# Comparing two Morton curves while the Hilbert keys are computed: one block for keys and ranks

## The chip, the cores and the metric

The kernel runs on one core of a Trainium2 chip. The metric is the device time of one execution in microseconds. TensorE (PE in the profile) multiplies matrices, VectorE (DVE) and ScalarE (ACT) work on tiles of 128 partitions, GpSimd (POOL) and SyncE (SP) are the others; transfers are issued from SP's and ACT's queues here.

## What is computed

The reference is a large model block: a graph attention over points, a Mamba block and a small feed-forward. The change touches its very first step alone, the sorting of 512 points in each of 16 batches along four space-filling curves:

```python
q = _quantize(coords_bn3)                 # 10 bits for each of 3 coordinates
qt = q[..., jnp.array([1, 0, 2])]
keys = [_morton_key(q), _morton_key(qt), _hilbert_key(q), _hilbert_key(qt)]
return [jnp.argsort(kk, axis=1) for kk in keys]
```

A Morton key interleaves the bits of x, y and z. A Hilbert key first transforms the coordinates bit by bit, nine rounds of and, or, xor and shifts, and then interleaves. The kernel doesn't sort: it computes for each point its rank, the number of points of its batch with a smaller key. Later stages gather neighbours by these ranks.

## The kernel before

B = 16 batches, N = 512 points, M = 4 methods (0 and 1 Morton, 2 and 3 Hilbert, each with x and y in order and swapped), NT = N / 128 = 4 tiles of points.

`norm_and_keys` (L93 to L349) is one block. DVE quantizes the coordinates (L237 to L261). SP stores the codes q to DRAM and loads them back over 128 partitions (L177, L179). DVE meanwhile does the layer norm of the latents (L266 to L273), for which ACT takes one square root (L224); SP stores the result to `f0` (L182). Then DVE copies the codes into A for the four methods (L285), works out the Hilbert transform for methods 2 and 3 (L286 to L311), and for all four methods together spreads the bits, puts the keys together and splits each into three parts in 16 bits (L313 to L329). SP stores all keys to `scratch["pk"]` (L185) and, after it has landed, SP loads methods 0 and 1 and ACT methods 2 and 3 into `mv_key` and `st_key` (L165): 16 transfers of 32 KB, each to one partition. The tile `p16` also has a row with the index (L172), four small loads. Eight transfers of 64 KB with constant rows ("units") go to the same two tiles from ACT's queue (L221), ahead of the square root in ACT's order. TensorE folds a convolution into two weight matrices (L195 to L203); DVE scales them after the keys (L331 to L343), TensorE transposes them (L208), DVE copies them (L348, L434, L435).

`ranks` (L352 to L420) is a second block. The four rows of a method lie on partitions 32m to 32m + 3. A product of four rows (L391), the sum of two halves, gives in a PSUM bank of 128 x 512 the difference of the keys of 128 points to all 512. Its sign is what counts: ACT takes methods 0 and 2 by `Sign` with a running sum (L419), DVE methods 1 and 3 by "less than" with a running sum (L406). A pair of comparisons, one for ACT and one for DVE, is issued together, half 0 of both and then half 1 of both:

```python
for half in range(2):
    for m in (2 * pair, 2 * pair + 1):
        last = nc.tensor.matmul(diff[:, t % 2, m, :],
                                st_key[32 * m:32 * m + 4, half, b, t * 128:t * 128 + 128],
                                mv_key[32 * m:32 * m + 4, half, b, 0:N],
                                start=half == 0, stop=half == 1)
```

There are 16 x 4 x 2 = 128 such pairs, 256 comparisons, 512 matmuls. A pair waits until ACT and DVE have both finished with the banks it writes (semaphores `signed`, `counted`); ACT and DVE wait for `compared`. At the end DVE turns ACT's sums into ranks (L409). The order on each engine is that of the code; `wait_ge` holds up all that is behind it on its engine. `link` makes each DVE instruction wait for the one before it. After the block, each block's semaphores are cleared, and `gather_windows` begins (its memsets on POOL, L557 on, its product of tokens, L622).

Of the kernel before, what the change touches and what calls it, by code (L numbers as in the profile page):

```python
# [6 lines left out]
F32 = mybir.dt.float32  # L7
F16 = mybir.dt.float16
# [84 lines left out]
def norm_and_keys(nc, io, scratch, mv_key, st_key, keys_in, weights, latn, fixed):  # L93

    with ExitStack() as ctx:
# [41 lines left out]
        pw = ctx.enter_context(nc.psum_tensor("pw", [128, 2, 4, 512], F32))  # L137
# [17 lines left out]
        turned = sem("w_turned")  # L155
        v_chain = sem("v_chain_keys")
# [3 lines left out]
        def load_keys(eng, m):  # L160

            for r in range(2):
                row = scratch["pk"][m, 2 * r:2 * r + 2, :].rearrange("(r h) (b n) -> r (h b) n", h=2, b=B)
                for tile, at in ((mv_key, 32 * m + r), (st_key, 32 * m + 2 + r)):
                    eng.dma_start(tile[at:at + 1, :, :, 0:N].rearrange("r h b n -> r (h b) n"), row).then_inc(keys_in, 16)  # L165

        @block.sync
        def _(sp):
            sp.dma_start(co[:, :], io["coords"]).then_inc(co_in, 16)
            sp.dma_start(lat[:, :, :], io["x"].rearrange("(t p) d -> p t d", p=128)).then_inc(lat_in, 16)  # L170
            for m in range(4):
# [4 lines left out]
            sp.wait_ge(q_ready, 1)  # L176
            sp.dma_start(scratch["q"], ci[:, :]).then_inc(q_out, 16)  # L177
            sp.wait_ge(q_out, 16)
            sp.dma_start(qin[:, :, :], scratch["q"].rearrange("(k b) n -> k (b n)", k=3)  # L179
                         .rearrange("k (p i) -> p k i", p=128)).then_inc(q_in, 16)  # L180
# [3 lines left out]
            sp.wait_ge(keys_ready, 3)  # L184
            sp.dma_start(scratch["pk"].rearrange("m r (p i) -> p (m r) i", p=128),  # L185
                         p16[:, :, :, :].rearrange("p m r i -> p (m r) i")).then_inc(keys_stored, 16)
            sp.wait_ge(keys_stored, 16)
            for m in (0, 1):
                load_keys(sp, m)
# [4 lines left out]
        def _(pe):  # L194
            pe.wait_ge(w_in, 16 * 7)  # L195
            for l in range(2):
                for m in range(M):
                    nc.tensor.matmul(pw[:, l, 0, 0:C], convT[:, l, :],
                                     lin[:, l, 0:128].rearrange("p (c m) -> p m c", m=M)[:, m, :],
                                     start=m == 0, stop=m == M - 1)  # L200
                nc.tensor.matmul(pw[:, l, 0, C:C + 128], convT[:, l, :], lin[:, l, 128:256], start=True, stop=True)
                nc.tensor.matmul(pw[:, l, 1, 0:1], convT[:, l, :], blin[:, l:l + 1], start=True, stop=True)\
                    .then_inc(folded, 1)  # L203
            for l, W in enumerate(weights):
                O = W["O"]
                pe.wait_ge(scaled, l + 1)
                for side in range(2):
                    last = nc.tensor.transpose(pw[:, l, 2 + side, 0:O],  # L208
                                               eff[0:O, l, side, :, :].rearrange("p c m -> p (c m)"), ident[0:O, 0:O])
                last.then_inc(turned, 1)  # L210

        @block.scalar
        def _(act):
# [16 lines left out]
        def _(dve):  # L230
# [51 lines left out]
            for e in range(2):  # L282
                for k in range(3):
                    src = qin[:, (k if e == 0 or k == 2 else 1 - k), :]
                    link(v.tensor_copy(turns[:, e, :, k, :], src.unsqueeze(1).to_broadcast([128, 2, P64])))  # L285
            ax = [A[:, 2:4, k, :] for k in range(3)]  # L286
# [26 lines left out]
            flat = A[:, :, :, :].rearrange("p m k i -> p (m k i)")  # L313
            flat2 = A2[:, :, :, :].rearrange("p m k i -> p (m k i)")
            for shift, mask in ((16, 0x030000FF), (8, 0x0300F00F), (4, 0x030C30C3), (2, 0x09249249)):
                link(v.scalar_tensor_tensor(flat2, flat, shift, flat, ALU.logical_shift_left, ALU.bitwise_or))
                link(v.tensor_scalar(flat, flat2, mask, None, ALU.bitwise_and))
            link(v.scalar_tensor_tensor(key[:, :, :], A[:, :, 0, :], 2, A[:, :, 2, :],
                                        ALU.logical_shift_left, ALU.bitwise_or))
            link(v.scalar_tensor_tensor(kp[:, :, :], A[:, :, 1, :], 1, key[:, :, :],  # L320
                                        ALU.logical_shift_left, ALU.bitwise_or))

            link(v.tensor_scalar(pi[:, 0, :, :], kp[:, :, :], 2 * BITS, None, ALU.logical_shift_right))
            link(v.tensor_scalar(pi[:, 1, :, :], kp[:, :, :], BITS, 2 ** BITS - 1, ALU.logical_shift_right,
                                 ALU.bitwise_and))
            link(v.tensor_scalar(pi[:, 2, :, :], kp[:, :, :], 2 ** BITS - 1, None, ALU.bitwise_and))
            link(v.tensor_copy(pf[:, :, :, :], pi[:, :, :, :]))
            for part, row, unit in ((0, 0, 32.0), (1, 2, 1.0 / 32.0), (2, 1, 1.0)):
                v.tensor_scalar(p16[:, :, row, :], pf[:, part, :, :], unit, None, ALU.mult).then_inc(keys_ready, 1)  # L329

            link(v.memset(eff[:, :, 0, :, :].rearrange("p l c m -> p l (c m)"), 0.0))  # L331
            for l, W in enumerate(weights):
                dve.wait_ge(folded, l + 1)
                link(v.tensor_copy(W["bias"][:, :], pw[:, l, 1, 0:1]))
                link(v.tensor_reduce(W["amax"][:, :], pw[:, l, 0, 0:C + 128], X, ALU.max, apply_absolute_value=True))
                link(v.tensor_scalar(W["amax"][:, :], W["amax"][:, :], 1e-30, None, ALU.max))
                link(v.reciprocal(inv[:, l:l + 1], W["amax"][:, :]))
                link(v.tensor_scalar(both[:, l, :], pw[:, l, 0, 0:C], inv[:, l:l + 1], None, ALU.mult))
# [4 lines left out]
                v.tensor_scalar(eff[:, l, 1, :, :].rearrange("p c m -> p (c m)"), pw[:, l, 0, C:C + 128],  # L343
                                inv[:, l:l + 1], None, ALU.mult).then_inc(scaled, 1)
            for l, W in enumerate(weights):
                O = W["O"]
                dve.wait_ge(turned, l + 1)
                link(v.tensor_copy(W["center"][:, 0:O], pw[:, l, 2, 0:O]))  # L348
                split16(v, link, W["neigh_hi"][:, 0:O], W["neigh_lo"][:, 0:O], pw[:, l, 3, 0:O])  # L349


def ranks(nc, io, scratch, rank, mv_key, st_key, keys_in):  # L352

    with ExitStack() as ctx:
        def sb(name, shape, dt=F32):
            return ctx.enter_context(nc.sbuf_tensor(name, shape, dt))

        used = []  # L360

        def sem(name):
            used.append(ctx.enter_context(nc.semaphore(name)))
            return used[-1]

        sign = sb("sign", [128, 4, N], F16)
        less = sb("less", [128, 4, N], F16)
        tally = sb("tally", [128, 2, B, NT])
        diff = ctx.enter_context(nc.psum_tensor("diff", [128, 2, M, 512], F32))

        used.append(keys_in)
        compared = sem("compared")
        signed = sem("signed")
        counted = sem("counted")
        scaled = sem("scaled_r")
        ctx.callback(clear, nc, used)
        block = ctx.enter_context(nc.Block())

        @block.tensor
        def _(pe):  # L380
            pe.sem_inc(signed, 4)
            pe.sem_inc(counted, 4)
            pe.wait_ge(keys_in, 16 * 6 * M)
            for b in range(B):
                for t in range(NT):
                    for pair in range(2):
                        pe.wait_ge(signed, b * (2 * NT) + (2 * t + pair + 1))
                        pe.wait_ge(counted, b * (2 * NT) + (2 * t + pair + 1))
                        for half in range(2):
                            for m in (2 * pair, 2 * pair + 1):  # L390
                                last = nc.tensor.matmul(diff[:, t % 2, m, :],  # L391
                                                        st_key[32 * m:32 * m + 4, half, b, t * 128:t * 128 + 128],
                                                        mv_key[32 * m:32 * m + 4, half, b, 0:N],
                                                        start=half == 0, stop=half == 1)
                                if half == 1:
                                    last.then_inc(compared, 1)

        @block.vector
        def _(dve):
            v = nc.vector  # L400
            with dve.Fori(0, B) as b:
                for t in range(NT):
                    for m in (1, 3):
                        dve.wait_ge(compared, b * (M * NT) + (t * M + m + 1))
                        dve.wait_ge(counted, b * (2 * NT) + (2 * t + m // 2 + 1))
# [1967 lines left out]
```

## Time and profile before

| | |
|---|---|
| median of 3 runs | 2323.17 us (2320.01 to 2326.31) |
| the profiled execution | 2328.78 us, its span 2327.0 us |
| keys, from the start to the first comparison | 99.60 us |
| ranks | 99.60 to 179.42 us |
| busy over the span | PE 81%, DVE 82%, ACT 69%, POOL 43% |

In the profile, a name such as "L391 PE MATMUL diff<-mv_key,st_key 4*128 4x512" is the line, the engine, the operation, what it writes and reads, and the shapes: weights of 4 x 128, moving data of 4 x 512. PEld is the loading of weights. A row of the timeline gives the start, the time to the end of what is merged in it, the count (x), and in brackets how long the engine had been idle and what it waited for. SPq and ACTq are the issuing of transfers. PEclk is the clock that the throttle granted to TensorE, as a share of 2.4 GHz.

### The profile page before, as it was taken

What the parts mean: (1) busy time and instruction counts of PE and PEld (TensorE: products, weight loads), DVE (VectorE), ACT (ScalarE), POOL (GpSimd) and SP (SyncE); (2) the same over time, 40 slices, a digit from 0 to 9 for tenths busy, and PEclk for the clock granted to TensorE, in tenths of its full rate; (3) what the DMA queues carried; (4) which work ended last, traced back from release to release, by engine and by line L of the source; (5) the groups of instructions that cost most, each with busy time, mean ns of one, the idle gap of its engine ahead of it and who ended that gap; (6) DMA issues with size and microseconds to landing.
All of it is one profiled execution on the core that took longest, in us unless ns stands there. A gap on an engine that the chain in (4) does not pass through costs nothing. (4 is left out here: it accounts for less than half of the span.)

```text
span 2327.0 us, 99837 instructions
## 1 busy us (share of the span) xinstructions
PE 1877.7 (81%) x37528; PEld 1288.0 (55%) x37528; DVE 1903.8 (82%) x3658; ACT 1616.3 (69%) x3249; POOL 1008.0 (43%) x995
## 2 busy tenths in 40 slices
PE   0296656888888566499999998577999999999948
PEld 0023335777777343389999996333544454445422
DVE  6798986999999599678989987874888888888854
ACT  0299986888888599689999997355455555555422
POOL 0000006999999100268787885002434344434401
PEclk9997668999999666699999998899999999999968
DMA  2103766555555177655555552202222222222110
GB/s 59 14 1 91 166 163 141 122 121 122 123 124 107 35 169 165 156 106 104 109 107 106 110 104 54 83 19 89 86 78 81 78 85 80 81 74 88 48 46 18
DMA packets 435513, 216.09 MB, mean 93 GB/s; under 512 B 301259, under 2 KB 404843, under 8 KB 435304
## 3 DMA queue, kind: packets, MB, share of 16 engines
q1 hardware_dynamic: 430120, 210.73, 38.2%
q10 hardware_dynamic: 5312, 4.31, 0.8%
q8 instruction: 47, 0.77, 0.1%
q14 instruction: 34, 0.28, 0.0%
HBM read 161.97 MB, written 52.96 MB: 92 GB/s over the span
## 5 line engine op out<-in xcount | busy, mean ns | idle before, releaser
L865 PE MATMUL pQ<-QM,QX 128*128 128x64 f16 (+1 forms) x5760 | 531.3, 217 | 2.1 <-issue 2.1
L863 PE MATMUL pQ<-neigh_lo,QX 128*128 128x32 f16 (+1 forms) x5760 | 519.6, 188 | 2.8 <-issue 2.8
L863 PEld LDWEIGHTS pQ<-neigh_lo,QX 128*128 128x128 f16 x5760 | 494.7, 103 | 6.5 <-issue 4.0
L865 PEld LDWEIGHTS pQ<-QM,QX 128*128 128x128 f16 x5760 | 486.6, 104 | 1.3 <-issue 1.2
L961 POOL TENSOR_TENSOR Dm<-Sc,mx 128x450 f32<-128x450 f32 x384 | 365.9, 953 | 79.9 <-DVE mx L921 79.9
L968 POOL TENSOR_TENSOR Ap<-E,R 128x450 f32<-128x450 f32 x384 | 366.0, 953 | 67.8 <-DVE R L934 57.4
L998 ACT ACTIVATE Vs<-pQ 128x480 f32<-128x480 f32 (+1 forms) x384 | 295.6, 770 | 5.4 <-PE pH L891 3.8
L930 DVE STREAM_TRANSPOSE AT<-Ap 128x480 f32<-128x480 f32 x384 | 259.1, 675 | 33.3 <-PE pH L891 10.9
L1963 POOL TENSOR_TENSOR MT<-cb,decay 128x512 f32 (+1 forms) x128 | 164.0, 1302 | 247.8 <-PEq L1731 151.1
L1011 ACT ACTIVATE E<-Dm 128x450 f32<-128x450 f32 x384 | 223.9, 583 | 60.3 <-POOL Dm L961 60.2
L921 DVE TENSOR_REDUCE mx<-Sc 128x15 f32<-128x450 f32 x384 | 223.9, 583 | 15.7 <-ACT Sc L992 15.4
L925 DVE TENSOR_REDUCE Z<-E 128x15 f32<-128x450 f32 x384 | 233.4, 608 | 0.0
L992 ACT ACTIVATE Sc<-pQ 128x450 f32<-128x450 f32 x384 | 208.8, 544 | 14.1 <-PE pQ L865 13.9
L891 PE MATMUL pH<-AT,Vs 128*32 128x30 f32 x17280 | 178.2, 197 | 48.2 <-DVE AT L930 42.6
L891 PEld LDWEIGHTS pH<-AT,Vs 128*32 128x32 f32 x17280 | 173.6, 110 | 68.3 <-DVE AT L930 42.0
L599 DVE TENSOR_TENSOR QT<-ext,cen 128x1710 f16<-128x1710 f32 x96 | 180.6, 1937 | 28.0 <-ACT ext L687 23.4
L858 PE MATMUL pQ<-maskR,maskL 128*128 128x160 f16 (+1 forms) x960 | 142.2, 246 | 69.0 <-DMA QX<-scratch_q 41.4
L1978 POOL TENSOR_TENSOR sqsum<-sqsum,sq 128x512 f32<-128x512 f32 x56 | 85.6, 1529 | 245.8 <-ACT sq L1824 245.8
L1756 PE MATMUL pO<-Wo,yw 128*128 128x512 f16 x768 | 179.7, 385 | 13.3 <-DVE Wo L1921 13.3
L1738 PE MATMUL pG<-h,W 128*128 128x512 f16 x768 | 178.6, 383 | 8.7 <-DVE W L1945 8.4
L1931 DVE SCALAR_TENSOR_TENSOR cv_m<-pX,taps_m,cv_m 128x496 f32<-128x496 f32 (+2 forms) x192 | 137.6, 717 | 51.0 <-ACT cv_m L1833 33.8
L1738 PE MATMUL pX<-h,W 128*128 128x512 f16 x768 | 176.2, 379 | 0.0
(360 smaller groups left out, 3592.2 us busy)
## 6 DMA issues: line engine op xcount, KB each, us to landing
QM<-scratch_q SPq DMA_DIRECT2D x192, 240.0 KB, 2.7
QX<-scratch_q SPq DMA_DIRECT2D x768, 60.0 KB, 2.4
scratch_q<-QT SPq DMA_DIRECT2D x120, 360.0 KB, 4.8
Wg<-in_in_proj SPq DMA_DIRECT2D x64, 256.0 KB, 2.6
Wh<-in_in_proj SPq DMA_DIRECT2D x64, 256.0 KB, 2.8
Wo<-in_out_proj SPq DMA_DIRECT2D x64, 256.0 KB, 2.6
W_s<-in_in_proj SPq DMA_DIRECT2D x16, 256.0 KB, 2.6
CT<-scratch_c SPq DMA_DIRECT2D x192, 11.2 KB, 2.1
```

The costliest lines, as they stand in the source:

```text
L863: nc.tensor.matmul(pQ[:, p, u // PB, o + 32:o + BW], qx[u], W["neigh_lo"][:, 0:O], start=False, stop=True, skip_group_check=True)
L865: last = nc.tensor.matmul(pQ[:, p, u // PB, o:o + BW], qx[u], qm[u], start=False, stop=True, skip_group_check=True)
L891: last = nc.tensor.matmul(pH[at0:at0 + 32, p, 32 * u:32 * u + PTS * K], Vs[:, first + slot, u * O + 32 * half:u * O + 32 * half + 32], AT[ ...
L921: v.tensor_reduce(mx[:, p, :], valid(Sc[:, p, :]), X, ALU.max).then_inc(max_ready, 1)
L925: v.tensor_reduce(Z[:, p, :], valid(E[:, p, :]), X, ALU.add).then_inc(summed, 1)
L930: v.transpose(AT[:, k5 % NA, :], A[:, k5 % ND, :]).then_inc(turned, 1)
L961: nc.gpsimd.tensor_tensor(valid(Dm[:, p, :]), valid(Sc[:, p, :]), mx[:, p, :].unsqueeze(2).to_broadcast([128, SUBS, PTS * K]), ALU.subtrac ...
L968: nc.gpsimd.tensor_tensor(valid(A[:, p, :]), valid(E[:, p, :]), R[:, p, :].unsqueeze(2).to_broadcast([128, SUBS, PTS * K]), ALU.mult).then ...
L992: nc.scalar.activation(like(Sc[:, (k - 1) % ND, :], 32, PTS * K), blocks(p, 0, PTS * K), ACT.Copy)\
L998: nc.scalar.activation(like(Vs[:, kv % RV, :], O, O), blocks(p, 32, O), ACT.Copy).then_inc(vs_ready, 1)
L1011: nc.scalar.activation(valid(E[:, p, :]), valid(Dm[:, p, :]), ACT.Exp, scale=32.0 ** -0.5).then_inc(exped, 1)
L1738: last = nc.tensor.matmul(out, W16[:, i, quarter, a, d, :], h16[:, b, d, :], start=d + a + b == 0, stop=d == DT - 1 and a == 1)
```

## The change

The two functions become one, `keys_and_ranks`, with one block.

- The first Morton methods come first: DVE spreads and splits methods 0 and 1 (`spread(0)`) ahead of the Hilbert transform, and methods 2 and 3 behind it (`spread(2)`). The key store is cut in two, and the key loads follow each: of the first half SP loads method 0 and ACT method 1, of the second SP loads both.
- The comparisons are dealt out anew. ACT takes all of methods 0 and 1 and batches 4 to 15 of method 2: 176. DVE takes batches 0 to 3 of method 2 and all of method 3: 80. The first 96 of ACT's list are issued two by two while DVE works on the Hilbert keys; the other 80 are issued each with one of DVE's.
- PSUM: `diff[:, 0]` is four banks for ACT, `diff[:, 1]` four for DVE. The folded weights lie in two banks of the latter; TensorE transposes them behind the 96, and waits for `taken` before DVE's comparisons write there.
- The eight loads of constant rows go behind the load of q on ACT, and behind the square root; on SP, the small loads (idx, rep, place, ident) go behind it.

```diff
@@ sync @@
             sp.dma_start(lat[:, :, :], io["x"]...).then_inc(lat_in, 16)
+            sp.wait_ge(q_ready, 1)
+            sp.dma_start(scratch["q"], ci[:, :]).then_inc(q_out, 16)
+            sp.wait_ge(q_out, 16)
+            sp.dma_start(qin[:, :, :], ...).then_inc(q_in, 16)
             for m in range(4):
                 sp.dma_start(p16[:, m, 3, :], io["idx"]).then_inc(idx_in, 16)
...
-            sp.wait_ge(keys_ready, 3)
-            sp.dma_start(scratch["pk"]...).then_inc(keys_stored, 16)
-            sp.wait_ge(keys_stored, 16)
-            for m in (0, 1):
-                load_keys(sp, m)
+            for half in range(2):
+                sp.wait_ge(keys_ready, 3 * half + 3)
+                sp.dma_start(scratch["pk"][2 * half:2 * half + 2]...).then_inc(keys_stored, 16)
+                sp.wait_ge(keys_stored, 16 * half + 16)
+                load_keys(sp, 2 * half)
+                if half == 1:
+                    load_keys(sp, 3)
@@ tensor @@
+            def difference(at, bank, m, b, t, half):
+                return nc.tensor.matmul(diff[:, at, bank, :], st_key[32 * m:32 * m + 4, half, b, t * 128:t * 128 + 128],
+                                        mv_key[32 * m:32 * m + 4, half, b, 0:N], start=half == 0, stop=half == 1)
+            def pair(jobs):
+                for at, n, m, b, t in jobs:
+                    pe.wait_ge((signed, counted)[at], n + 1)
+                for half in range(2):
+                    for at, n, m, b, t in jobs:
+                        last = difference(at, n % 4, m, b, t, half)
+                        if half == 1:
+                            last.then_inc(compared[at], 1)
+            signs = [(0, n) + job for n, job in enumerate([(m, b, t) for m in range(3) for b in range(SHARED if m == 2 else 0, B)
+                                                           for t in range(NT)])]
+            counts = [(1, n) + job for n, job in enumerate([(m, b, t) for m in (2, 3) for b in range(SHARED if m == 2 else B)
+                                                            for t in range(NT)])]
+            pe.sem_inc(signed, 4)
+            pe.sem_inc(counted, 4)
+            pe.wait_ge(keys_in[0], 16 * 12)
+            for n in range(0, ALONE * NT, 2):
+                pair(signs[n:n + 2])
             for l, W in enumerate(weights):
                 pe.wait_ge(scaled, l + 1)
...
+            pe.wait_ge(taken, 2)
+            pe.wait_ge(keys_in[1], 16 * 12)
+            for one, two in zip(signs[ALONE * NT:], counts):
+                pair((one, two))
@@ scalar @@
+            act.wait_ge(var_ready, 1)
+            nc.scalar.activation(sd[:, :], mv[:, :, 1], ACT.Sqrt).then_inc(sd_ready, 1)
+            act.wait_ge(q_in, 16)
             for m in range(M):
                 for tile, side, at in ((mv_key, 0, 32 * m + 2), (st_key, 1, 32 * m)):
                     act.dma_start(tile[at:at + 2, :, :, 0:N]..., io["units"][side])\
-                        .then_inc(keys_in, 16)
-            act.wait_ge(var_ready, 1)
-            nc.scalar.activation(sd[:, :], mv[:, :, 1], ACT.Sqrt).then_inc(sd_ready, 1)
+                        .then_inc(keys_in[m // 2], 16)
             act.wait_ge(keys_stored, 16)
-            for m in (2, 3):
-                load_keys(act, m)
+            load_keys(act, 1)
+            def jobs(m, b0, b1, before):
+                with act.Fori(b0, b1) as b:
+                    for t in range(NT):
+                        n = b * NT + (t + before - b0 * NT)
+                        act.wait_ge(compared[0], n + 1)
+                        act.wait_ge(signed, n + 1)
+                        nc.scalar.activation(sign[:, t, :], diff[:, 0, t, :], ACT.Sign,
+                                             accum_out=tally[:, m, bass.ds(b, 1), t]).then_inc(signed, 1)
+            jobs(0, 0, B, 0)
+            jobs(1, 0, B, B * NT)
+            jobs(2, SHARED, B, 2 * B * NT)
@@ vector @@
+            spread(0)
             ax = [A[:, 2:4, k, :] for k in range(3)]
...
+            spread(2)
...
+                dve.sem_inc(taken, 1)
+            jobs(2, SHARED, 0)
+            jobs(3, B, SHARED * NT)
+            dve.wait_ge(signed, (3 * B - SHARED) * NT + 4)
```

`ALONE` is 24 and `SHARED` 4. DVE's `jobs` is as ACT's, with `is_lt`, `diff[:, 1, t, :]`, `compared[1]` and `counted`. `spread(m)` is the code of L313 to L329 on the two methods m and m + 1.

## Rows read from the trace of the kernel before

**Rows 1.** Busy us by stage: PE, PEld, DVE, ACT, POOL, clock, DMA share, GB/s.
```profile
0.00:99.60 99.60, 6.16 (x28) 5.76 (x28) 68.16 (x224) 1.49 (x2) 0.20 (x4) 1.00 0.22 42
99.60:179.40 79.80, 78.21 (x512) 20.47 (x512) 78.44 (x257) 77.75 (x256) 0.00 (x0) 1.00 0.00 1
```
**Rows 2.** Timeline of the keys: start us, us, engine, line, what.
```profile
11.65 0.33 SPq L177 DMA_DIRECT2D scratch_q<-ci  x1
...
29.60 1.53 DVE L285 COPY A<-qin 128x128 int32<-128x128 int32 x6 [8.04 <-DMA qin<-scratch_q]
...
73.90 0.96 DVE L316 SCALAR_TENSOR_TENSOR A<-A 128x768 int32<-128x768 int32 x1
...
80.24 0.43 DVE L318 SCALAR_TENSOR_TENSOR key<-A 128x256 int32<-128x256 int32 x1
...
83.44 0.27 DVE L331 MEMSET eff<- 128x256 f32 x1
...
86.75 0.59 SPq L165 DMA_DIRECT2D mv_key<-scratch_pk  x1
...
99.60 2.00 PE L391 MATMUL diff<-mv_key,st_key 4*128 4x512 f16 x16 [10.96 <-DMA st_key<-scratch_pk]
```
**Rows 3.** Timeline of the ranks: ACT near their start, DVE near their end.
```profile
104.55 0.59 ACT L419 ACTIVATE sign<-diff 128x512 f16<-128x512 f32 x1
...
105.12 0.60 ACT L419 ACTIVATE sign<-diff 128x512 f16<-128x512 f32 x1
...
172.47 0.69 DVE L406 TENSOR_SCALAR_CACHE_REDUCE less<-diff 128x512 f16<-128x512 f32 x1
...
173.08 0.69 DVE L406 TENSOR_SCALAR_CACHE_REDUCE less<-diff 128x512 f16<-128x512 f32 x1
...
179.19 0.23 DVE L409 TENSOR_SCALAR rank<-tally 128x128 f32<-128x128 f32 x1
```
**Rows 4.** TensorE: durations (ns min/median/max), then timeline and clock of two tail stretches.
```profile
L391 PE MATMUL diff<-mv_key,st_key x512: 577/626/630, 99.6 to 177.4; 4*128 4x512 f16 x171
...
L2253 PE MATMUL pu_f<-W_f,uf_f x18: 379/412/635, 2314.7 to 2321.2; 115*128 115x512 f16 x18
...
2302.79 4.00 PE L2253 MATMUL pg_f<-W_f,uf_f 115*128 115x512 f16 x9 [1.37 <-DVE la_f L2182]
...
2319.48 2.12 PE L2253 MATMUL pu_f<-W_f,uf_f 115*128 115x512 f16 x9
...
2302.80:2312.70 9.90, 9.90 (x21) 0.50 0.07 26
...
2318.00:2321.80 3.80, 3.80 (x14) 0.98 0.17 65
```
**Rows 5.** Timeline of two early weight loads of the ranks.
```profile
100.00 0.26 PEld L391 LDWEIGHTS diff<-mv_key,st_key 4*128 4x128 f16 x4 [0.16 <-issue]
...
100.43 0.26 PEld L391 LDWEIGHTS diff<-mv_key,st_key 4*128 4x128 f16 x4 [0.17 <-issue]
```
**Rows 6.** Timeline of the square root's table load, here and at L1090.
```profile
16.72 1.28 ACT L224 ACT_TABLE_LOAD   x1 [16.72 <-issue]
...
772.22 1.28 ACT L1090 ACT_TABLE_LOAD   x1 [2.13 <-PEq L53]
```
**Rows 7.** Transfers: KB and us to landing; DMA share and GB/s of one stretch.
```profile
co<-in_coords SPq DMA_DIRECT2D x1, 96.0 KB, 2.3
scratch_q<-ci SPq DMA_DIRECT2D x1, 96.0 KB, 8.0
qin<-scratch_q SPq DMA_DIRECT2D x1, 96.0 KB, 9.9
...
15.00:17.50 2.50, 1.00 0.14 23
```
**Rows 8.** Timeline of the last copies of the folded weights.
```profile
88.75 0.23 DVE L348 CAST center<-pw 128x64 f16<-128x64 f32 x1
...
89.27 0.22 DVE L435 TENSOR_TENSOR neigh_lo<-pw,neigh_hi 128x64 f16<-128x64 f32 x1
```

More of the change, by code:

```diff
@@ L90, in chain, with keys_and_ranks @@
     return link
-def norm_and_keys(nc, io, scratch, mv_key, st_key, keys_in, weights, latn, fixed):
+def keys_and_ranks(nc, io, scratch, rank, mv_key, st_key, weights, latn, fixed):
     with ExitStack() as ctx:
@@ L136, in norm_and_keys @@
         inv = sb("inv", [128, 2])
-        pw = ctx.enter_context(nc.psum_tensor("pw", [128, 2, 4, 512], F32))
+        sign = sb("sign", [128, 4, N], F16)
+        less = sb("less", [128, 4, N], F16)
+        tally = sb("tally", [128, 3, B, NT])
+        diff = ctx.enter_context(nc.psum_tensor("diff", [128, 2, 4, 512], F32))
+        pw = diff[:, 1, 0:2, :]
+        BIAS, TURN = 192, 256
+        ALONE = 24
+        SHARED = 4
         lat_in = sem("lat_in")
@@ L155, in norm_and_keys @@
         turned = sem("w_turned")
+        taken = sem("w_taken")
+        keys_in = [sem("keys_in0"), sem("keys_in1")]
+        compared = [sem("compared_a"), sem("compared_v")]
+        signed = sem("signed")
+        counted = sem("counted")
         v_chain = sem("v_chain_keys")
@@ L347, in _ @@
                 dve.wait_ge(turned, l + 1)
[L348 to L405, printed above, removed]
-                        v.tensor_scalar(less[:, (2 * t + m // 2) % 4, :], diff[:, t % 2, m, :], 0.0, 0.0, ALU.is_lt,
-                                        ALU.add, accum_out=rank[:, bass.ds(b + m * B, 1), t]).then_inc(counted, 1)
-            dve.wait_ge(signed, B * 2 * NT + 4)
-            v.tensor_scalar(rank[:, :, :].rearrange("p (a c) t -> p a c t", a=2)[:, :, 0:B, :], tally[:, :, :, :],
-                            -0.5, (N - 1) / 2.0, ALU.mult, ALU.add).then_inc(scaled, 1)
-        @block.scalar
-        def _(act):
-            with act.Fori(0, B) as b:
-                for t in range(NT):
-                    for m in (0, 2):
-                        act.wait_ge(compared, b * (M * NT) + (t * M + m + 1))
-                        act.wait_ge(signed, b * (2 * NT) + (2 * t + m // 2 + 1))
-                        nc.scalar.activation(sign[:, (2 * t + m // 2) % 4, :], diff[:, t % 2, m, :], ACT.Sign,
-                                             accum_out=tally[:, m // 2, bass.ds(b, 1), t]).then_inc(signed, 1)
@@ new lines, in _, with jobs @@
+                link(v.tensor_copy(W["center"][:, 0:O], pw[:, l, TURN:TURN + O]))
+                split16(v, link, W["neigh_hi"][:, 0:O], W["neigh_lo"][:, 0:O], pw[:, l, TURN + 128:TURN + 128 + O])
+                dve.sem_inc(taken, 1)
+            def jobs(m, b1, before):
+                with dve.Fori(0, b1) as b:
+                    for t in range(NT):
+                        n = b * NT + (t + before)
+                        dve.wait_ge(compared[1], n + 1)
+                        dve.wait_ge(counted, n + 1)
+                        v.tensor_scalar(less[:, t, :], diff[:, 1, t, :], 0.0, 0.0, ALU.is_lt, ALU.add,
+                                        accum_out=rank[:, bass.ds(b + m * B, 1), t]).then_inc(counted, 1)
@@ L1281, in cross_attention @@
             mv_key, st_key = (kctx.enter_context(nc.sbuf_tensor(n, [128, 2, B, N + 2], F16)) for n in ("mv_key", "st_key"))
[L1282 to L1284 removed]
+            keys_and_ranks(nc, io, scratch, rank, mv_key, st_key, weights, latn, fixed)
         f0 = scratch["f0"].rearrange("(a p) n -> p a n", p=128)
```

70 lines of the change are left out of this document (35 added, 35 removed).

## The prediction

> **What bounds the kernel now.** The view by stage comes first [rows 1]. Everything the change touches lies before 179.4 us of a span of 2327.0 us; nothing after it is edited. Up to 99.6 us DVE works and TensorE and ACT all but rest; from 99.6 to 179.4 us all three read as full. The change fills the first stretch with work of the second, so the question is which engine sets the pace once that work is split otherwise.
>
> In order of time [rows 2]: q is stored at 11.65 us and comes back before 29.60; DVE then needs 29.60 to 73.90 us for copies and Hilbert keys and 9.54 us more (to 83.44) for spreading bits and splitting keys. The key loads are issued from 86.75 us on, and the first comparison starts at 99.60.
>
> In the ranks [rows 3] DVE starts a comparison every 0.611 us (172.47, 173.08), with no gap; 128 of them are 78.2 us, and the rank tile is written at 179.42. ACT, when it has input, starts one every 0.57 us (104.55, 105.12) [rows 3]. So DVE bounds this phase today.
>
> TensorE looks as if it kept up easily, and that reading needs care. Its 512 matmuls last 577 to 630 ns, median 626 [rows 4]. The tail of the kernel shows the same width of 512 columns at both clock levels: at a granted clock of 0.50 (1.2 GHz) the nine matmuls from 2302.79 take 4.00 us; at 0.98 (2.4 GHz) the nine from 2319.48 take 2.12 us. Single ones of that line last 379 to 412 ns at the upper level and 635 at the lower [rows 4]. The view by stage prints 1.00 for the ranks, but no matmul there is under 577 ns. I go by the instructions: the ranks run at the lower level from beginning to end. Price of one 512-column matmul among others on the same array rows: (4.00 - 0.18) / 9 = 0.424 us at 1.2 GHz, (2.12 - 0.17) / 9 = 0.217 us at 2.4 GHz, weight load hidden in both; about 0.18 us is what the duration of the last one has over its 512 columns (635 and 379 ns against 427 and 213).
>
> Two early weight loads of the ranks say it again [rows 5]: with buffers free, new weights go in at 100.00 and again at 100.43, a step of 0.43 us, the time of 512 columns at 1.2 GHz. Yet 16 matmuls are done in 2.00 us [rows 2]. 16 x 0.427 is 6.8 us, so about four run at a time: methods 0 to 3 sit on partitions 0, 32, 64 and 96, and alternate pairs use (0, 1) and (2, 3). Each method gets two matmuls (0.854 us) in every 2 x 0.611 = 1.22 us. **Only because four separate groups of rows share the work does TensorE at 1.2 GHz not bound the ranks.**
>
> **The change, part by part.**
>
> *Comparisons alone, 96 of them.* `pair` takes two successive entries of `signs`, both of method 0 (64 jobs) or both of method 1 (32). All four matmuls of a pair, and those of the next pair, stand on one group of rows and run one after the other. A job costs two, 2 x 0.427 = 0.854 us, against 0.57 us for ACT. TensorE bounds: 96 x 0.854 = 82.0 us. Four banks don't add to it: a pair waits for the ACT job two places before the preceding pair's end, and ACT (0.57 us and 0.2 us of reading) is done with it well inside the 1.71 us that the preceding pair streams.
>
> *Comparisons shared, 80 pairs.* They are methods (1, 2) x16, (1, 3) x16 and (2, 3) x48. Two groups of rows run side by side, but the next pair stands on the same two: 0.854 us a pair, over DVE's 0.611 and ACT's 0.57. 80 x 0.854 = 68.3 us. At 2.4 GHz it would be 0.43, and DVE would bound: 48.9 us.
>
> Does the clock level change? Before the ranks TensorE idled 11 us; during them its busy row is full for 78 us with up to four groups of rows at work [rows 1, 3], and the durations never fall. After the change one or two groups work. I see nothing that would lift it, and take 1.2 GHz. Beside that stands the Trainium skill, "TensorE: Matmul & The Clock Gate", Part 1: a busy engine is lifted to 2.4 GHz. The matmuls of the ranks (626 ns to the end) do not agree. By that rule the change would win; it is a rival below.
>
> *The keys' front.* ACT's Sqrt waited for a table load at 16.72, behind ACT's eight loads of constant rows (L221); at L1090 the table load goes as soon as the block has started, ahead of the wait for DVE [rows 6]. With the constants moved, it goes at about 5.3 us; `sd` is ready 0.2 us after 15.5, not at 18.21: 2.5 us gained, and the layer norm ends near 19.0. The q store took 8.0 us and the load back 9.9 with those constants in flight [rows 7]; co's 96 KB took 2.3 [rows 7]. At 2.3 to 3.5 us each q is back at 16 to 19 us, and costs DVE nothing. DVE starts its copies near 19.0 instead of 29.60, ends them at 20.6, and `spread(0)` follows.
>
> *Two spreads for one.* A shift-or takes 0.96 us on 768 elements and 0.43 on 256 [rows 2]: 1.03 ns an element and 0.165 us, and 0.033 to the next instruction, so 0.2 us that don't shrink. A spread is 17 instructions, 9.54 us on all four methods. On two it is (9.54 + 17 x 0.2) / 2 = 6.5 us, both 13.0. Morton keys are ready at 27.1, Hilbert keys at 27.1 + 42.7 + 6.5 = 76.3 us.
>
> *Where the constants go.* They now start at about 17 us, when q is in. With next to nothing else in flight, from 15 to 17.5 us, the transfers run at a share of 0.14 and 23 GB/s [rows 7], some two of 16 engines; 8 x 64 KB at 23 to 24 GB/s is 22 us. So they now last from about 18.5 to at least 40 us, longer with what shares those engines: f0, and the first key store at 27.1. ACT's loads of method 1's keys queue behind them. Floor for the first keys: 40 + 1.5 = 41 us. Ceiling: constants stretched by f0 and the key store to 49, and then all 8 key loads at 9 us (16 took 12.8 from issue to first matmul): 58. Between these I take 49, the queue delays near those of q and f0 in the trace (8.0 and 9.9 us). SP's idx, rep, place and ident move behind q; only the first key store needs idx, and it is later anyway.
>
> *The rest.* The second key store goes at 76.3, its eight loads all on SP (4.9 us of issuing); done by some 92, hidden under the comparisons until 131; the cover is 39 us deep, and without it every us that the keys come after 131 would count in full. DVE's weight folding (L331 to L343, 4.6 us) is hidden likewise. Behind the 96 jobs TensorE turns the weights and waits for `taken`: four transposes and DVE's six small operations, 2.1 us, estimated from [rows 8]: 0.74 for the copies of the wider matrix (88.75 to 89.49), a little less for the other, and half a us for transposes and hand-overs. ACT and DVE are idle there. The removed block border lay under the key loads' 11 us: nothing. End: drain, last comparison and two scalings, 1.6 us.
>
> **Sum.** 49 + 82.0 + 2.1 + 68.3 + 1.6 = 203.0 us for the ranks, against 179.4: +23.6 us. The profiled execution is 2328.78 us (span 2327.0), 5.6 above the median of 2323.17; on its own scale it would become 2352.4, on the median's 2346.8. I forecast the median's scale: **2347 us**.
>
> **Rivals.**
>
> A (forecast): 1.2 GHz, TensorE bounds both parts. With the start at 41 or 58 us instead of 49: 2338.8 to 2355.8.
>
> B: TensorE at 2.4 GHz (faster, the other side). ACT bounds the part alone (96 x 0.57 = 54.7), DVE the shared one (48.9): 49 + 54.7 + 2.1 + 48.9 + 1.5 = 156.2, so -23.2 us: 2300. It decides wherever a matmul lasts under 0.57 / 2 us; for it speaks only the printed 1.00, against it every duration in the ranks. 8 in 100.
>
> C: 1.2 GHz alone, 2.4 GHz once two groups work: -19.4 against A, 2327.6, within the noise. Before, two to four groups did not lift it. 3 in 100.
>
> D: weight loads not hidden on one group of rows: 0.1 us for each of 192 + 160 matmuls in line, +35: 2382. Rows of [rows 4] and [rows 5] speak against it. The Trainium skill, "TensorE: Matmul & The Clock Gate", Part 3, says a weight load overlaps running matmuls only where the group of rows differs; the nine at 0.424 us have one each and do not agree. 3 in 100.
>
> E: the change does not do what it says, and comparisons and Hilbert keys do not overlap. The folded weights (`pw`) lie in `diff[1]`, the signs go to `diff[0]`, so no bank couples them; only first keys that come after 76.3 us would undo the overlap. That needs 18 us beyond the ceiling; it has no chance of its own here.
>
> A has 86 in 100. **Range** 2336 to 2358: A's bounds with 2 to 3 us for the spread of the runs. About 0.3% (7 us) is what a measurement here tells from no change. Slower by more: A and D, 0.89. Within: C, 0.03. Faster: B, 0.08.
>
> **What would show it.** Matmuls of the ranks again at 600 ns and more; TensorE full and ACT idle between signs, with a step of 0.85 us a job and 0.85 us a pair; ranks starting at 41 to 58 us and ending near 203; DVE idle from about 80 to 131 us; Sqrt's table load near 5 us; q back before 19. Wrong it would be if matmuls fall to about 0.4 us, if ACT starts one every 0.57 us with TensorE waiting for it, or if the first keys land before 41 us by far.

## The result and the profile after

The changed kernel takes 2349.63 us (median of 4 runs, 2342.08 to 2353.24), the kernel before 2324.74 (4 runs, those of the first table and one more). The ratio is 1.0096, 95% interval 1.0078 to 1.0114: slower by 1%, as forecast. The profiled execution of the changed kernel has a span of 2351.3 us against 2327.0.

The view by stage of the changed kernel, columns as in [rows 1]; its stages are keys up to the first comparison, comparisons alone, comparisons shared:

```profile
0.00:49.97 49.97, 5.28 (x25) 5.20 (x25) 41.99 (x138) 1.49 (x2) 0.20 (x4) 1.00 0.35 76
49.97:131.90 81.93, 81.93 (x196) 27.68 (x196) 27.69 (x99) 60.18 (x191) 0.00 (x0) 1.00 0.03 5
131.90:201.60 69.70, 67.26 (x322) 26.47 (x320) 56.87 (x167) 55.22 (x164) 0.00 (x0) 1.00 0.00 0
```

The first comparison comes 50 us earlier than in [rows 2], and still the ranks end 22 us later. TensorE is full for 82 us and then busy for 67 of 70, while ACT and DVE are not. The bound has moved from DVE to TensorE. The rows of its two instructions (ns min/median/max) and who waited for them:

```profile
L220 PEld LDWEIGHTS diff<-mv_key,st_key x512: 97/146/147, 50.0 to 199.4; 4*128 4x128 f16 x171
L220 PE MATMUL diff<-mv_key,st_key x512: 578/629/629, 50.0 to 199.9; 4*128 4x512 f16 x171
...
  ACT sign L278: 69.7, 120
  DVE less L421: 10.1, 55
```

The matmuls are as long as in [rows 4], so the clock level is the same. What changed is who waits: ACT 120 times for a comparison, where it waited once before (for its very first), and DVE 55 times. The timeline shows the pace, first alone, then shared:

```profile
49.97 0.13 PEld L220 LDWEIGHTS diff<-mv_key,st_key 4*128 4x128 f16 x2 [36.49 <-DMA st_key<-scratch_pk]
...
50.37 0.15 PEld L220 LDWEIGHTS diff<-mv_key,st_key 4*128 4x128 f16 x1 [0.28 <-issue]
...
50.80 0.15 PEld L220 LDWEIGHTS diff<-mv_key,st_key 4*128 4x128 f16 x1 [0.28 <-issue]
...
51.23 0.15 PEld L220 LDWEIGHTS diff<-mv_key,st_key 4*128 4x128 f16 x1 [0.28 <-issue]
...
135.42 0.69 DVE L421 TENSOR_SCALAR_CACHE_REDUCE less<-diff 128x512 f16<-128x512 f32 x1
...
136.27 0.69 DVE L421 TENSOR_SCALAR_CACHE_REDUCE less<-diff 128x512 f16<-128x512 f32 x1
...
137.12 0.69 DVE L421 TENSOR_SCALAR_CACHE_REDUCE less<-diff 128x512 f16<-128x512 f32 x1 [0.15 <-PE diff L220]
...
201.43 0.18 DVE L429 TENSOR_SCALAR rank<-tally 128x48 f32<-128x48 f32 x1
```

One weight load every 0.427 us, one at a time, each beside the running matmul: that is the part alone, on one group of rows. In [rows 5] each such step carried several. In the shared part DVE starts every 0.85 us where it did every 0.611 in [rows 3].

The same trace has two short stretches in which a third group of rows works. They stand where the methods of the pairs change, from (1, 2) to (1, 3) and from (1, 3) to (2, 3). At the first, two of the steps carry three loads instead of two:

```profile
145.26 0.15 PEld L220 LDWEIGHTS diff<-mv_key,st_key 4*128 4x128 f16 x2 [0.28 <-issue]
145.68 0.15 PEld L220 LDWEIGHTS diff<-mv_key,st_key 4*128 4x128 f16 x3 [0.27 <-ACT sign L278]
146.11 0.15 PEld L220 LDWEIGHTS diff<-mv_key,st_key 4*128 4x128 f16 x3 [0.28 <-issue]
```

There and again from 159.32 us on, three steps in a row start three matmuls instead of two. The trace does not name the group, but by their number the third is the first of the incoming group, beside the two at work. So the 320 matmuls of the shared part need 157 steps of 0.427 us instead of 160, and behind the second change DVE starts a few comparisons every 0.61 us (161.66, 162.28, 162.89, 163.50 us).

### The profile page after: what moved, and what is told of

Read it like the earlier page. It is cut to its first block and busy times, and to the rows that moved or that the text cites. A ratio compares the mean times of both kernels' runs of the same rounds, so it can differ in the third digit from the quotient of the medians.

```text
span 2351.3 us, 99904 instructions
## 1 busy us (share of the span) xinstructions
PE 1959.5 (83%) x37528; PEld 1326.1 (56%) x37528; DVE 1884.2 (80%) x3580; ACT 1654.7 (70%) x3345; POOL 1007.3 (43%) x995
## 5 line engine op out<-in xcount | busy, mean ns | idle before, releaser
L978 POOL TENSOR_TENSOR Ap<-E,R 128x450 f32<-128x450 f32 x384 | 365.8, 953 | 68.3 <-DVE R L944 58.1
L1002 ACT ACTIVATE Sc<-pQ 128x450 f32<-128x450 f32 x384 | 209.1, 544 | 15.7 <-PE pQ L875 15.7
L868 PE MATMUL pQ<-maskR,maskL 128*128 128x160 f16 (+1 forms) x960 | 143.2, 247 | 68.3 <-DMA QX<-scratch_q 41.0
L220 PE MATMUL diff<-mv_key,st_key 4*128 4x512 f16 x512 | 148.8, 626 | 37.7 <-DMA st_key<-scratch_pk 36.4
```

The lines of the kernel that those rows point to most:

```text
L978: nc.gpsimd.tensor_tensor(valid(A[:, p, :]), valid(E[:, p, :]), R[:, p, :].unsqueeze(2).to_broadcast([128, SUBS, PTS * K]), ALU.mult).then ...
L1002: nc.scalar.activation(like(Sc[:, (k - 1) % ND, :], 32, PTS * K), blocks(p, 0, PTS * K), ACT.Copy)\
```

## The experiments

Each ratio is to the kernel before, measured on the same chip at the same time. From one such measurement to another the median of the kernel before differs by up to 4 us (2325 above, 2326 to 2329 below). The end of the ranks, read from each timeline, carries most of the argument, as nothing behind it is changed: 179.4 us before, 201.6 after.

**Is it the groups of rows? In the old kernel alone.** The order of the pairs changes, and with it which of the banks a comparison is written to; no key comes earlier.

```diff
-            for b in range(B):
-                for t in range(NT):
-                    for pair in range(2):
+            for b in range(B):
+                for pair in range(2):
+                    for t in range(NT):
...
-                                last = nc.tensor.matmul(diff[:, t % 2, m, :],
+                                last = nc.tensor.matmul(diff[:, m % 2, t, :],
```

> The kernel before, with one thing changed: the order of its pairs. In each batch the four pairs of methods (0, 1) come first and then the four of (2, 3), so that successive pairs stand on the same two groups of array rows; as many matmuls, comparisons and banks as before, no key made earlier. My theory (a group of rows takes one 512-column matmul in 0.427 us, so a pair whose neighbours use the same rows costs 0.854 us): 128 pairs last 109.3 us instead of 78.2, the ranks end near 210.5, and the time is 31 us over that of before, about 2356. Rival (the groups of rows don't matter; the pace of a pair comes from the hand-over of banks or from DVE): 0.611 us a pair, 2325.

Measured: 2337.53 us, ratio 1.0053 (1.0033 to 1.0073), and the ranks end at 188.1 us instead of 179.4. That is 11 us in time and 9 in the ranks, neither 31 nor 0. The order alternates every four pairs, and there are four banks each for ACT and DVE: while the last pair on (0, 1) runs, pairs on (2, 3) can start beside it, and the timeline shows steps of 0.61 and of 0.86 us mixed. My number left this out. So the order was taken to its end, with all of (0, 1) first and then all of (2, 3):

```diff
-            for b in range(B):
-                for t in range(NT):
-                    for pair in range(2):
+            for pair in range(2):
+                for b in range(B):
+                    for t in range(NT):
...
-                                last = nc.tensor.matmul(diff[:, t % 2, m, :],
+                                last = nc.tensor.matmul(diff[:, m % 2, t, :],
```

> The kernel before, with the order of its pairs changed further than in the run before: all 64 pairs of methods (0, 1) and then all 64 of (2, 3), so that no pair of the other groups of rows is near. Where the order alternated every four pairs, four banks were enough to work on both at once, and the cost was 11 us instead of 31. My theory: now 128 pairs at 0.854 us, 109.3 instead of 78.2, ranks end near 210, time 31 us over that of before, about 2356. Rival (the cost of the run before was one of changing groups every four pairs, not of sharing rows): under 11 us now, 2325 to 2337.

Measured: 2357.48 us, ratio 1.012 (1.0101 to 1.0139), against 2328.57 of before: 29 us. The ranks end at 209.3 us, 30 later. From the view by stage of this kernel, and then its timeline:

```profile
99.60:209.00 109.40, 108.19 (x512) 41.05 (x512) 88.92 (x255) 87.51 (x256) 0.00 (x0) 1.00 0.00 1
```

```profile
150.82 0.69 DVE L406 TENSOR_SCALAR_CACHE_REDUCE less<-diff 128x512 f16<-128x512 f32 x1 [0.15 <-DVE less L406]
...
151.67 0.69 DVE L406 TENSOR_SCALAR_CACHE_REDUCE less<-diff 128x512 f16<-128x512 f32 x1 [0.15 <-DVE less L406]
...
209.09 0.23 DVE L409 TENSOR_SCALAR rank<-tally 128x128 f32<-128x128 f32 x1
```

The same 512 matmuls and 256 comparisons take 109 us instead of 79.8 [rows 1], at 0.85 us a pair, with successive pairs on the same rows. No transfer and no wait of the change is in this kernel, so the order alone is enough for a loss of this size. Both runs here also deal out the banks anew; the next one leaves the banks as they are and changes only the rows.

**Two groups of rows in the part alone.** In the changed kernel ACT's Morton jobs are taken in turn:

```diff
-            signs = [... for job in enumerate([(m, b, t) for m in range(3) ...])]
+            signs = [... for job in enumerate([(m, b, t) for b in range(B) for t in range(NT) for m in (0, 1)] + ...)]
```

> The changed kernel, with one thing changed: ACT's two Morton methods are dealt in turn (0, 1, 0, 1, ...), so that each of the pairs issued alone stands on two groups of rows instead of one. Same jobs alone (96), same jobs shared (80). My theory: two matmuls side by side make 0.427 us a job, ACT's own 0.57 to 0.58 bounds, the part alone shrinks from 82 to about 56 us, the shared part stays at 68, ranks end near 177, and the time is 24 to 26 us under the changed kernel's: about 2325. Rival (the part alone is paced by TensorE's issue or by the wait for two free banks): 0.85 us a job as before, 2350.

Measured: 2327.41 us, ratio to before 1.0006 (0.9993 to 1.0018), about 22 us under the changed kernel. The part alone takes 61 us (49.4 to 110.3). ACT's starts:

```profile
53.09 0.60 ACT L285 ACTIVATE sign<-diff 128x512 f16<-128x512 f32 x1
...
53.67 0.59 ACT L285 ACTIVATE sign<-diff 128x512 f16<-128x512 f32 x1
...
54.24 0.60 ACT L285 ACTIVATE sign<-diff 128x512 f16<-128x512 f32 x1
...
54.47 0.16 PEld L220 LDWEIGHTS diff<-mv_key,st_key 4*128 4x128 f16 x4 [1.23 <-ACT sign L285]
...
54.83 0.59 ACT L285 ACTIVATE sign<-diff 128x512 f16<-128x512 f32 x1
...
55.63 0.60 ACT L285 ACTIVATE sign<-diff 128x512 f16<-128x512 f32 x1
```

Three steps of 0.57 to 0.59 and one of 0.80 us, 2.54 us for four jobs, 0.636 each. The long one is the wait of a pair for two free banks. Expected were 56 us; the groups of rows are worth 21 of the 82, and this wait keeps 5 more (the last run below takes it away). The banks are dealt out as in the changed kernel, so they are not the cause of the 21.

**Fewer jobs alone.** If a job alone costs TensorE as much as a shared pair of two, jobs should be moved into pairs:

```diff
-        ALONE = 24
-        SHARED = 4
+        ALONE = 12
+        SHARED = 10
```

> The changed kernel with other numbers alone: ALONE 12 instead of 24 batches and SHARED 10 instead of 4, so 48 jobs alone and 104 shared pairs. My theory (TensorE bounds both parts, a job alone costs 0.854 us and a shared pair of two jobs costs as much): alone 41 us, from 50 to 91, when the Hilbert keys have landed (their transfers end near 86); shared 88.8; ranks end at 50 + 41 + 1.5 + 88.8 + 1.6 = 183, 18.6 us earlier than in the changed kernel: about 2331. Rival (DVE's pace or late Hilbert keys bound the shared part): more shared pairs gain less than half of that or cost time, 2341 or more.

Measured: 2327.41 us, ratio 0.9995 (0.9985 to 1.0004). The shared part starts at 92.74 us and the ranks end at 181.4, 20.2 us before the changed kernel's; 18.6 were expected. The sum by 0.854 us holds at another split too.

**The constants.** First the constants, the square root and SP's small loads go back where they were (the lines for SP are left out here):

```diff
+            for m in range(M):
+                for tile, side, at in ...: act.dma_start(..., io["units"][side])
             act.wait_ge(var_ready, 1)
             nc.scalar.activation(sd[:, :], mv[:, :, 1], ACT.Sqrt).then_inc(sd_ready, 1)
-            act.wait_ge(q_in, 16)
-            for m in range(M):
-                for tile, side, at in ...: act.dma_start(..., io["units"][side])
```

> The changed kernel with the eight constant loads, the square root and SP's small loads in the order of before. My theory: this part of the change gives nothing to the first keys, since the constants only move from under the codes to under the first key store, which they held for 10.6 us. With them ahead again, codes are back at 29.6, the first keys are stored from 37.7 in about 3 us and loaded by about 50; comparisons start within 2 us of the changed kernel's 50.0, the Hilbert keys come 10 us later under cover, and the time is within 3 us of 2350. Rival (the earlier codes carry through): the first comparison starts 8 to 10 us later, and the time is about 2359.

Measured: 2351.86 us, ratio 1.0111 (1.0087 to 1.0134), first comparison at 52.15 us instead of 49.97. With the constants behind the codes DVE starts its copies 10.9 us earlier (19.10 against 30.04), but the key store takes most of it back: 10.6 us to landing in the changed kernel, 2.3 here (38.03 to 40.30). Then only half of them moved on, behind the first key loads:

```diff
-            for m in range(M):
+            for m in (0, 1):
                 ... act.dma_start(..., io["units"][side])
...
+                else:
+                    for m in (2, 3):
+                        ... sp.dma_start(..., io["units"][side])
```

> The changed kernel with the constant rows of methods 2 and 3 (four of the eight loads) moved once more: to SP, behind the first key store and method 0's key loads. My theory (the first key store took 10.6 us because it stood among the constants): the four loads left are through by about 30 us, the store lands in about 3 to 5 us instead of 10.6, comparisons start at 41 to 44 instead of 50; TensorE bounds all that follows, so the whole gain arrives: 6 to 9 us, about 2342. Rival (the store was slow because of f0's 1 MB, which was issued 8 us before it): start at 48 or later, time within 2 us of 2350.

Measured: 2342.32 us, ratio 1.0059 (1.0045 to 1.0072). Of this kernel, f0 and the key store in the list of DMA issues (KB, us to landing), and the first product in the timeline:

```profile
scratch_f<-latn SPq DMA_DIRECT2D x1, 1024.0 KB, 11.1
...
scratch_pk<-p SPq DMA_DIRECT2D x1, 128.0 KB, 3.9
```

```profile
42.86 3.59 PE L225 MATMUL diff<-mv_key,st_key 4*128 4x512 f16 x8 [29.12 <-DMA st_key<-scratch_pk]
```

The same list of DMA issues of the changed kernel:

```profile
scratch_f<-latn SPq DMA_DIRECT2D x1, 1024.0 KB, 11.5
...
scratch_pk<-p SPq DMA_DIRECT2D x1, 128.0 KB, 10.6
scratch_q<-ci SPq DMA_DIRECT2D x1, 96.0 KB, 1.9
qin<-scratch_q SPq DMA_DIRECT2D x1, 96.0 KB, 2.0
```

The transfer of f0 is as in the changed kernel (11.1 and 11.5 us, issued 8 us ahead of the key store in both), the store is 6.7 us faster, the comparisons start 7.1 us earlier, and the ranks end at 194.5 instead of 201.6: all of it arrives, as TensorE bounds from there on. It was the constants that held the store, not f0.

**The clock.** A product over all 128 rows ahead of each pair:

```diff
+                at, n = jobs[0][0:2]
+                nc.tensor.matmul(diff[:, at, n % 4, 0:extra], fixed["place"][:, 0:128], fixed["place"][:, 0:extra],
+                                 start=True, stop=True)
...
+            pe.wait_ge(fixed_in, 48)
```

> The changed kernel plus one product over all 128 rows ahead of each pair, whose result is overwritten: 512 columns for the pairs alone, 256 for the shared ones. My theory of the clock (it stays at 1.2 GHz because the comparisons use only four rows of each group): with it TensorE rises to 2.4 GHz, matmuls last about 0.38 us, a pair alone costs 5 x 0.213 = 1.07 us and ACT bounds at 1.14, a shared pair 0.53 and DVE bounds at 0.61: 50 + 56 + 2 + 49 + 2 = 159 us for the ranks, 2307 in all. Rival (it stays at 1.2 GHz whatever the rows do): 2.13 us for a pair alone, 102 us; 1.07 for a shared one, 85 us; ranks end near 240, about 2388.

Measured: 2417.09 us, ratio 1.0394 (1.0374 to 1.0414). The comparisons' matmuls stay at 602 to 629 ns, the lower level. So one full-height product per pair does not raise it, and my theory of why the level is low found no support; what 2.4 GHz would be worth is not tested. The time is longer than even the rival said (2388), and the timeline says where:

```profile
52.34 0.61 PE L228 MATMUL diff<-place 128*128 128x512 f16 x1
...
52.88 1.88 PE L220 MATMUL diff<-mv_key,st_key 4*128 4x512 f16 x4
...
54.70 0.61 PE L228 MATMUL diff<-place 128*128 128x512 f16 x1
```

A pair alone costs 2.36 us where five matmuls are 2.13. The first comparison starts 0.54 us after the full product (its 512 columns are 0.43), and the next full product 1.82 us after that (four matmuls are 1.71): 0.11 us each way. A shared pair costs 1.29 us where its matmuls are 1.07. So going from four-row products to a full one and back costs 0.22 to 0.23 us. 48 and 80 times that is 29 us, just what is missing.

Then a warm-up instead: 110 such products back to back while TensorE waits for the first keys.

```diff
+            pe.wait_ge(fixed_in, 48)
+            for n in range(110):
+                nc.tensor.matmul(diff[:, 0, n % 4, :], fixed["place"][:, 0:128], fixed["place"][:, 0:512],
+                                 start=True, stop=True)
             pe.wait_ge(keys_in[0], 16 * 12)
```

> The changed kernel plus 110 products over all 128 rows, 512 columns each, while TensorE waits for the first keys (results overwritten). They should reach the 2.4 GHz level within themselves (durations near 0.38 us) and end about when the first keys are there. Then the comparisons show whether they hold that level. One theory (the level follows how busy TensorE is): they hold it, matmuls of 0.38 us throughout, ACT bounds at 0.57 us a job alone, ranks end near 160, 2308. Other (these four-row products don't hold it): a few us of comparisons at 0.38 us, then 0.63 again; ranks end at most 3 us earlier than 201.6, or later by what the products overrun; 2345 to 2353.

Measured: 2346.07 us (one run), ranks ending near 200.4. Its timeline, and then its stages, columns as in [rows 1]:

```profile
39.76 9.01 PE L241 MATMUL diff<-place 128*128 128x512 f16 x41
49.96 1.90 PE L220 MATMUL diff<-mv_key,st_key 4*128 4x512 f16 x8 [1.19 <-DMA st_key<-scratch_pk]
```

```profile
40.00:50.00 10.00, 8.81 (x42) 3.82 (x41) 8.98 (x31) 0.00 (x0) 0.00 (x0) 1.00 0.42 18
51.90:53.00 1.10, 0.68 (x2) 0.28 (x3) 1.00 (x4) 1.10 (x5) 0.00 (x0) 0.50 0.00 0
53.00:130.00 77.00, 77.00 (x185) 25.50 (x183) 24.77 (x89) 57.30 (x182) 0.00 (x0) 0.50 0.03 6
```

The 41 full products take 0.22 us each (2.4 GHz). TensorE then waits 1.19 us for the keys, and the first eight comparison matmuls are through in 1.90 us (four jobs; 3.6 us at the lower level). By 51.9 us, as these eight end, the granted clock already reads 0.50, and it stays there with TensorE full to 130 us. So in this kernel the throttle's own record puts the comparisons at 1.2 GHz too.

The first of the 110 products show what a printed 1.00 is worth before that record begins:

```profile
24.00:27.00 3.00, 3.00 (x8) 1.06 (x7) 2.73 (x12) 0.00 (x0) 0.00 (x0) 1.00 0.14 33
29.00:39.00 10.00, 10.00 (x48) 4.57 (x47) 8.98 (x31) 0.00 (x0) 0.00 (x0) 1.00 0.15 32
```

Eight products of 512 columns in 3 us is the pace of 1.2 GHz (one every 0.427 us, 24.07, 24.50 and 24.93 us), 48 in 10 us that of 2.4 GHz, and the column prints 1.00 for both. The 1.00 in the ranks of the other kernels also stands before the first recorded change of the clock; in the kernel before, the column first reads less than 1.00 at 198 us. The run does not say what would keep the level up: the fall comes after a short wait and with four-row products, and nothing here separates the two.

**All four groups.** If the groups of rows are the cause, a deal of jobs by rows should beat both kernels: methods 0 and 1 in turn alone, then triples of pairs (0, 2), (1, 3), (2, 3).

```diff
+        order_a, order_v = list(alone), []
+        while later:
+            order_a += [later.pop(0), later.pop(0), h2a.pop(0)]
+            order_v += [h2v.pop(0), h3.pop(0), h3.pop(0)]
```

> The changed kernel with its jobs dealt by groups of rows: 72 jobs alone with methods 0 and 1 in turn; then 28 times the three pairs (0, 2), (1, 3), (2, 3) and 8 pairs (2, 3); TensorE turns the weights 8 jobs before the end of the part alone, so that nobody waits for it. ACT's and DVE's jobs are written out instead of looped. My theory: alone 0.636 us a job (as with two groups above), 45.8; 84 pairs at DVE's 0.611 and 8 at 0.854, 58.2; ranks end at 50 + 45.8 + 58.2 + 1.6 = 155.6, 46 us before the changed kernel's: about 2303, 1% faster than before. Rival (mixed pairs still meet on a group and cost 0.854, or the written-out code of ACT and DVE stalls): shared part 78 us or more, 2323 or more.

Measured: 2299.11 us, ratio 0.9866 (0.9845 to 0.9886): 1.3% faster than before, 2.1% faster than the changed kernel. DVE's steps, in the triples and in the last pairs on (2, 3), and the end:

```profile
99.87 0.69 DVE L423 TENSOR_SCALAR_CACHE_REDUCE less<-diff 128x512 f16<-128x512 f32 x1
...
100.49 0.69 DVE L423 TENSOR_SCALAR_CACHE_REDUCE less<-diff 128x512 f16<-128x512 f32 x1
...
147.98 0.69 DVE L423 TENSOR_SCALAR_CACHE_REDUCE less<-diff 128x512 f16<-128x512 f32 x1 [0.15 <-PE diff L234]
148.84 0.69 DVE L423 TENSOR_SCALAR_CACHE_REDUCE less<-diff 128x512 f16<-128x512 f32 x1 [0.16 <-PE diff L234]
...
153.00 0.17 DVE L428 TENSOR_SCALAR rank<-tally 128x36 f32<-128x36 f32 x1
```

0.61 us where four groups share the work, 0.86 where two do, in one kernel. The ranks end at 153.2 us; 155.6 were expected.

Last, the comparisons alone one by one, with 64 of them:

```diff
-            for n in range(0, ALONE * NT - 8, 2):
-                pair(signs[n:n + 2])
+            for n in range(ALONE * NT - 6):
+                pair(signs[n:n + 1])
```

> The kernel of the run with four groups, with two changes: the comparisons alone are issued one by one (each waits for one free bank, not for two), and there are 64 of them instead of 72, with 32 triples (0, 2), (1, 3), (2, 3) behind. My theory (with two groups of rows in turn only the wait for two banks kept ACT from its own pace): 0.572 us a job alone, 50 to 87 us; 96 pairs at 0.611; ranks end near 147, 6 us before the 153.1 of that kernel; about 2293. Rival (one job at a time gets no overlap between jobs, 0.85 us each): part alone until 104, ranks end at 164, 2310.

Measured: 2296.99 us, ratio 0.9865 (0.985 to 0.988), no different in time from the run before it; the ranks end at 150.1 instead of 153.2 in the profiled execution, and 147 was expected. ACT now keeps its 0.57 us (52.21, 52.78, 53.35), and the missing 3 us are the Hilbert keys:

```profile
90.01 3.60 PE L234 MATMUL diff<-mv_key,st_key 4*128 4x512 f16 x23 [2.77 <-DMA st_key<-scratch_pk]
```

I had put them at 86 us, by the last activity of their transfers; what waits for them starts at 90. Their 39 us of cover in the changed kernel is here below zero.

## Why the prediction was right

It said 2347 us, in 2336 to 2358, and 2349.6 came. Step by step:

- *Which stage, and who bounds it.* The ranks end at 201.6 us, 203.0 was the sum. TensorE bounds both parts, at 1.2 GHz. The order experiment shows the cause in the old kernel, with no other part of the change present (29 us of 31), and taking the rows in turn gives 22 us back in the new one.
- *Alone, 82.0 us.* The last job's matmuls end at 131.6, 81.6 us after the first: right to half a us, which is one step saved where method 0 gives way to method 1. Two groups of rows in the same place give 61.
- *Shared, 68.3 us.* The matmuls take 67.0 us (133.34 to 200.3), because the prediction left out the two changes of methods, at which a third group of rows works for three steps. The end behind them is 1.3 us instead of 1.6. The gap between the parts was 1.7 us instead of 2.1; TensorE took the first two transposes in between, ahead of the last comparisons, so that only two were left behind them.
- *The front.* Table load at 5.25 us (5.3), `sd` at 15.84 (15.7), copies from 19.10 (19.0). The q store and load took 1.9 and 2.0 us, under the 2.3 to 3.5 that I had allowed; DVE was still at the layer norm, so nothing hung on it. A spread took 6.3 us, 6.5 was worked out; the Hilbert keys were stored at 76.0 (76.3).
- *The constants.* The first comparison came at 49.97 (49): the store was issued at 27.1, landed after 10.6 us, close to the delays of [rows 7], and the keys took 12.3 us more. The store's delay is the right reason: with all constants ahead the comparisons start at 52.15, with half of them later at 42.86, and what the change does with the constants is worth 2 us. But the prediction nowhere adds 49 up, and one price beside it was wrong. It gave eight key loads 9 us in its ceiling; from issue to first matmul they took 12.3, and 11.85 in both of the other runs, hardly less than the 12.8 of sixteen. With 9 the same sum would give 46.7. That the point was met within 1 us is in part luck; that the bounds of 41 and 58 held is not.
- *After the ranks.* The end of the ranks moved by 22.2 us, the first product of the next stage by 22.7 (182.20 to 204.87), the span by 24.3. The last 1.6 us I did not trace; it is less than the runs differ among themselves.
- *Rival B* (2.4 GHz) fell by the durations, 578 to 629 ns in the changed kernel. The throttle's own record confirms the level only after the warm start, where it reads 0.50 from 51.9 us on. The rival's price could not be measured, since nothing tried held the upper level. *Rival D* (weight loads in line) fell by the timeline: a load each 0.427 us beside a running matmul on the same rows, and nothing added to the 0.427. The Trainium skill, "TensorE: Matmul & The Clock Gate", Part 3, says that a weight load overlaps running matmuls only where the group of rows differs; this trace does not agree. *Rival C* fell with the shared part's 0.85. *E* did not come up: DVE was done with its keys under ACT's comparisons as the change means it to be.

What the change wanted was there: comparisons start 50 us earlier and DVE's key work is hidden whole. It was paid for on TensorE: 82 us for 96 of the 256 comparisons and 67 for the other 160, where all of them took 80 before.

## What to carry to other kernels

Before an engine's work is dealt out anew, price it on TensorE by groups of array rows: products of few rows are cheap only while neighbours stand on other groups, and a new order can undo this with the same instructions. Read TensorE's level from the durations of its matmuls beside others of the same width, not from the clock column alone, which printed 1.00 for both levels here. Do not read the bound from a full busy column either: it was full in [rows 1], where TensorE had time to spare, and full when it was the bound. A load moved out of the way of one transfer stands in the way of the next one; look at what comes behind it.

## What the hardware showed beyond this

With four banks for each engine and an order that alternates every four pairs, TensorE works on both sets of row groups part of the time: the ranks end 9 us later instead of 30, at 0.61 and 0.86 us a pair mixed. Going from four-row products to a 128-row one and back costs 0.22 us each time. The eight loads of 64 KB to two partitions move some 23 GB/s together, and while they are in flight a store of 96 or 128 KB on another queue takes 8.0 and 10.6 us instead of 1.9 and 2.3; four of them, issued 9 to 11 us ahead of it, delayed it by at most 2 (3.9 against 2.3 us). Eight loads of 32 KB to one partition each took 11.8 to 12.3 us from the first issue to the first matmul, sixteen 12.8. And the comparisons did not stay at the upper clock level after a warm start: the record reads 0.50 with TensorE full.
